# A state-space layer and a mixture of experts on one core: x1 on VectorE in the step of its output, experts chosen a step sooner

## The reference, cut to what matters

```python
z = irfft(rfft(x') * rfft(K)) + x' * D        # x' = layernorm(x); K is built from the S4D parameters
out = layernorm(x' + z) * ln_w + ln_b
x1 = x + layernorm(out)
zn = layernorm(layernorm(x1)) * ln_g + ln_b   # then the FFN
w = top-2 of softmax(zn @ rW + rb), over 8 experts
mixed = sum_e w_e * (gelu(zn @ W1_e + b1_e) @ W2_e + b2_e)
result = x1 + layernorm(layernorm(x1) + mixed)
```

## Time and profile before

| | |
|---|---|
| median of 3 runs | 642.32 us (641.46 to 644.99) |
| the profiled execution | 644.5 us, its span 642.9 us |
| granted TensorE clock, mean | 0.878 of full speed |
| busy in the span | PE 75%, VectorE 76%, ScalarE 51%, GpSimd 41% |

### The profile page before, as it was taken

How to read it: one execution, slowest core, us unless ns; L and a number is a source line. 1 busy time by engine, 2 the same in 40 slices (tenths; PEclk the granted TensorE clock), 3 DMA queues, 4 the chain that set the end, 5 groups by cost and what they waited for, 6 DMA issues and landing times. The chain is left out here.

```text
span 642.9 us, 12334 instructions
## 1 busy us (share of the span) xinstructions
PE 484.8 (75%) x2809; PEld 418.0 (65%) x2810; DVE 488.9 (76%) x1426; ACT 329.3 (51%) x646; POOL 262.4 (41%) x205
## 2 busy tenths in 40 slices
PE   0479899848997773600189999999999999992970
PEld 0239888736876663600078888888888889892760
DVE  7997959889988977884057778777777787770796
ACT  6974721353455366620055555555555555545485
POOL 0001586545776665788503223322332323233420
PEclk9998999968987985555579999999999999995995
DMA  6106500100110657642432222222222222215963
GB/s 198 66 0 262 197 1 0 66 1 9 59 68 33 229 197 216 227 139 74 153 118 68 81 66 82 66 82 66 82 67 80 66 82 72 75 49 212 346 229 145
DMA packets 36826, 69.55 MB, mean 108 GB/s; under 512 B 7520, under 2 KB 23648, under 8 KB 36160
## 3 DMA queue, kind: packets, MB, share of 16 engines
q1 hardware_dynamic: 30320, 51.48, 24.3%
q0 software_dynamic: 6480, 17.77, 7.7%
HBM read 42.02 MB, written 27.21 MB: 108 GB/s over the span
## 5 line engine op out<-in xcount | busy, mean ns | idle before, releaser
L1165 POOL DMA_INDIRECT y_rows<-y_sb,dst x71 | 76.6, 1079 | 192.7 <-DVE y_sb L1056 149.9
L1340 PE MATMUL psum<-ws,z_hl 128*128 x426 | 119.8, 417 | 0.8 <-DVE z_hl L1033 0.8
L1359 PE MATMUL psum<-ws,h_hl 128*128 x852 | 116.0, 286 | 0.1
L1359 PEld LDWEIGHTS psum<-ws,h_hl 128*128 128x128 f32 x852 | 103.6, 189 | 0.3 <-issue 0.3
L1147 POOL DMA_INDIRECT z_rows<-zn,pos x64 | 76.9, 1201 | 30.6 <-issue 17.7
L1340 PEld LDWEIGHTS psum<-ws,z_hl 128*128 128x128 f32 x426 | 76.7, 192 | 16.0 <-issue 1.5
L591 ACT CAST h_hl<-psum 128x512 fp32r<-128x512 f32 x71 | 41.7, 587 | 75.8 <-PE psum L1349 75.8
L1041 DVE TENSOR_TENSOR hb<-psum,b1r 128x512 f32<-128x512 f32 x71 | 49.1, 691 | 37.5 <-issue 34.0
L583 ACT ACTIVATE z_f<-psum,gb 128x128 f32<-128x128 f32 x142 | 57.0, 452 | 32.8 <-PE psum L1327 31.1
L1232 PE MATMUL psum<-pm,ft 128*128 128x256 f32 x256 | 65.7, 418 | 0.4 <-DVE tmp L836 0.4
L1327 PE MATMUL psum<-ident,z_in 128*128 128x128 f32 x142 | 28.6, 284 | 43.9 <-DMA z_in<-z_rows 42.0
(11 more groups left out here) (200 smaller groups left out, 874.7 us busy)
## 6 DMA issues: line engine op xcount, KB each, us to landing
z_in<-z_rows SPq DMA_DIRECT2D x71, 129.0 KB, 2.1
w_raw<-in_dram SPq DMA_DIRECT2D x16, 512.0 KB, 4.9
ya<-y_rows SPq DMA_DIRECT2D x16, 512.0 KB, 6.1
xs<-in_dram SPq DMA_DIRECT2D x8, 512.0 KB, 5.4
x_dram<-xs SPq DMA_DIRECT2D x8, 512.0 KB
x1m<-x_dram SPq DMA_DIRECT2D x2, 2048.0 KB, 8.4
out_dram<-acc SPq DMA_DIRECT2D x8, 512.0 KB, 2.6
b1r<-in_dram SPq DMA_DIRECT2D x8, 256.0 KB
```

The lines of the kernel that those rows point to most:

```text
L1165: pool.indirect_dma_start(y_rows, bass.IndirectOffsetOnAxis(ap=dst[q][:, 0:1], axis=0), y_sb[q][:, :], None).then_inc(sem(f"y_out{q}"), 16)
L1340: last = TE.matmul(ps_h[q], z_hl[q][:, a, k], w_at(e1, c, k * F, F), start=n == 0, stop=n == 5)
L1359: last = TE.matmul(ps_y[q], h_hl[q][:, a, k], w_at(e2, c, 1024 + k * H, H), start=n == 0, stop=n == 11)
```

## The change

- **x1** is made on VectorE in the step of its output: four `scalar_tensor_tensor` of 256 columns compute o*rs + x and at once sum their result into `st` (`accum_out`). The additive term (mean of o times rs) isn't applied there; it is kept in `xb` and added in the mixing stage by one more small operation per row. `dl` on ScalarE and the addition on GpSimd (L1139) go.
- **Statistics** of o and x1: the sums come with the operation that writes them (the addition of ln_b becomes four such operations too); the squares about the mean are summed by ScalarE (`ACT.Square` with `accum_out`, four per tensor). The eight bn_stats and eight bn_aggr per row for these two go. Those of r stay.
- **Routing a step sooner**: zn is written in the step of x1, tail is n-2. `choose` stands at the end of a step, `place` and the ranks in the next one, behind the statistics of r; in step 8 both follow for row 6 at once, and row 7 is chosen in step 9. rb and the regions' starts are added by two small TensorE matmuls; `lgs`, `posf`, `posr` go, and the copy of `tok` moves to ScalarE.
- **GpSimd**: the second half of `combine` moves to the start of the next step, the first waits for o; five scatters stand before it, three behind.
- **Weights**: the casts and subtractions move (the tables below); GpSimd makes none. A Gelu on one element is put before the tile loop on ScalarE.
- **SP**: the wait for the last scatters moves behind the pads.

```diff
@@ SP @@
             behind = [sp.value_load(padi[0:1, e:e + 1], min_val=0, max_val=ROWS - P) for e in range(E)]
-            for i in (2, 3):
-                sp.wait_ge(sem(f"scattered{i}"), 128)
             for e in range(E):
                 sp.dma_start(z_rows[bass.ds(behind[e], P), :], zpad[:, :]).then_inc(sem("pads"), 16)
...
             sp.wait_ge(sem("pads"), 16 * E)
+            for i in (2, 3):
+                sp.wait_ge(sem(f"scattered{i}"), 128)
             load_z(0, 0)
@@ ScalarE: renormalise, step @@
-                sigma(mid, 3)
-                act.wait_ge(sem("st_x1"), mid.b + 1)
+                act.wait_ge(sem("x1_mean"), row.b + 1)
+                for k in range(4):
+                    last = nc.scalar.activation(dump[:, k], xs[row.b][:, k], ACT.Square, bias=mv1[:, row.b, k, 0:1],
+                                                accum_out=mv1[:, row.b, k, 1:2])
+                last.then_inc(sem("var3"), 1)
+                sigma(row, 3)
+                act.wait_ge(sem("st_x1"), row.b + 1)
...
-                if n == B:
-                    renormalise(mid)
+                for e in HIGH.get(n, ()):
+                    split_high(e)
                 if cur.live:
-
+                    act.wait_ge(sem("o_mean"), cur.b + 1)
+                    for k in range(4):
+                        last = nc.scalar.activation(dump[:, k], o[:, k], ACT.Square, bias=mv[1][:, k, 0:1],
+                                                    accum_out=mv[1][:, k, 1:2])
+                    last.then_inc(sem("var1"), 1)
                     sigma(cur, 1)
-                    act.wait_ge(sem("st_o"), cur.b + 1)
-                    if not cur.first():
-                        act.wait_ge(sem("x1_ready"), cur.b)
-                    for k in range(4):
-                        last = nc.scalar.activation(dl[:, k], o[:, k], ACT.Identity, bias=rs[:, 1, 4 + k:5 + k],
-                                                    scale=rs[:, 1, k:k + 1])
-                    last.then_inc(sem("dl_ready"), 1)
...
-                if mid.live and n != B:
-                    renormalise(mid)
-                for e in HIGH.get(n, ()):
-                    split_high(e)
+                if cur.live:
+                    renormalise(cur)
@@ VectorE: step @@
+                if last_tail.live and n != B + 1:
+                    place(last_tail)
...
                 if n == B:
-                    mid_now()
+                    choose(tail)
...
-                    do(V.tensor_tensor(o[:, :, :], o[:, :, :], lwb[:, 1].unsqueeze(1).to_broadcast([P, 4, H]), ALU.add))
-                    stats(lambda k: o[:, k], 1)
+                    for k in range(4):
+                        last = V.scalar_tensor_tensor(o[:, k], o[:, k], 1.0, lwb[:, 1], ALU.mult, ALU.add,
+                                                      accum_out=st[:, 1, 0, k:k + 1])
+                    last.then_inc(sem("o_ready"), 1)
+                    dve.wait_ge(sem("o_ready"), cur.b + 1)
+                    V.tensor_scalar(mv[1][:, :, 0], st[:, 1, 0, 0:4], -1.0 / H, None, ALU.mult).then_inc(sem("o_mean"), 1)
                 if nxt.live:
                     mult(nxt, 1)
+                if n == B:
+                    place(tail)
                 if cur.live:
                     do(inverse(cur, 1))
...
+                    for k in range(4):
+                        last = V.scalar_tensor_tensor(xs[cur.b][:, k], o[:, k], rs[:, 1, k:k + 1], xs[cur.b][:, k], ALU.mult,
+                                                      ALU.add, accum_out=st[:, 3, 0, k:k + 1])
+                    last.then_inc(sem("x1_ready"), 1)
...
+                if tail.live and n != B:
+                    choose(tail)
+                if cur.live:
+                    do(inverse(cur, 3))
+                    V.tensor_tensor(rs[:, 3, 4:8], mv1[:, cur.b, :, 0], rs[:, 3, 0:4], ALU.mult).then_inc(sem("st_x1"), 1)
@@ VectorE: scale, in the mixing stage @@
-                       ALU.mult).then_inc(sem("m_rs"), 1)
+                       ALU.mult).then_inc(sem("m_sh"), 1)
+                dve.wait_ge(sem("m_sh"), b + 1)
+                gate(dve)
+                V.tensor_tensor(rm[:, par, 2, :], rm[:, par, 2, :], xb[:, bass.ds(back(b), 1)].rearrange("p a k -> p (a k)"),
+                                ALU.add).then_inc(sem("m_rs"), 1)
@@ GpSimd: step @@
+                if cur.live and cur.b:
+                    if cur.b > 1:
+                        pool.wait_ge(sem("st_x1"), cur.b - 1)
+                    combine(cur, 1)
+                if last_tail.live and n != B + 1:
+                    scatter(last_tail, 0, 5)
                 if nxt.live:
+                    if nxt.b > 1:
+                        pool.wait_ge(sem("o_ready"), nxt.b - 1)
                     combine(nxt, 0)
-                    combine(nxt, 1)
+                    if nxt.b == 0:
+                        combine(nxt, 1)
+                if last_tail.live and n != B + 1:
+                    scatter(last_tail, 5, 8)
+                if n == B:
+                    scatter(tail, 0, 8)
...
-                if cur.live:
-                    pool.wait_ge(sem("dl_ready"), cur.b + 1)
-                    G.tensor_tensor(xs[cur.b][:, :, :], xs[cur.b][:, :, :], dl[:, :, :], ALU.add).then_inc(sem("x1_ready"), 1)
@@ the tables @@
-HIGH = {3: (0,), 4: (1,), 5: (2,), 6: (3,), 7: (4,), 9: (5,), 10: (6,)}
-LOW = {9: (0,), 10: (1,), B + LAG: (4, 5, 6, 7)}
-LOW_POOL = {B + LAG: (2, 3)}
+HIGH = {0: (0, 1), 1: (2,), 4: (3,), 7: (4,), 8: (5, 6)}
+LOW = {1: (0, 1), 2: (2,), 8: (3,), 9: (4, 5, 6), B + LAG: (7,)}
```

More of the change, by code:

```diff
@@ L872, in place @@
                 for c in range(2):
[L873 removed]
+                    last = V.tensor_tensor(prod[:, c], oh[:, c], route(row.b)[1][:, 64:96].rearrange("p (t e) -> p t e", t=4),
+                                           ALU.mult)
                 do(last)
[L875 removed]
                 if not row.first(2):
                     dve.wait_ge(sem(f"scattered{row.par}"), 64 * min(row.b - row.par, 6))
[L878 removed]
@@ L879, in place @@
                 V.tensor_copy(zn[buf(row.b)][:, :, H + 1], mif[:, 1])
-                V.tensor_copy(pos[row.par][:, :, :], posr[:, :, :]).then_inc(sem("pos_ready"), 1)
+                with nc.allow_low_precision(reason="one term of each sum is not zero, and it is a whole number"):
+                    V.tensor_reduce(pos[row.par][:, :, :], prod[:, :, :, :], AX.X, ALU.add).then_inc(sem("pos_ready"), 1)
             def step(n):
-                nxt, cur, mid, tail = (Row(n, k) for k in (1, -1, -2, -LAG))
@@ L884, in mid_statistics @@
-                def mid_statistics():
-                    for k in range(4):
-                        last = V.bn_aggr(mv1[:, mid.b, k, :], st[:, 3, k, :])
-                    last.then_inc(sem("var3"), 1)
-                def mid_scales():
-                    if not mid.first():
-                        dve.wait_ge(sem("zn_ready"), mid.b)
-                    do(inverse(mid, 3))
-                    V.scalar_tensor_tensor(rs[:, 3, 4:8], mv1[:, mid.b, :, 0], -1.0, rs[:, 3, 0:4], ALU.mult,
-                                           ALU.mult).then_inc(sem("st_x1"), 1)
@@ L1277, in step @@
             def step(n):
-                nxt, cur, tail = Row(n, 1), Row(n, 0), Row(n, -LAG)
+                nxt, cur, tail, last_tail = (Row(n, k) for k in (1, 0, -2, -LAG))
+                if last_tail.live:
+                    pe.wait_ge(sem("mask_ready"), last_tail.b + 1)
+                    rank = route(last_tail.b)[1][:, 64:96]
+                    m = mask[:, :, :].rearrange("p t e -> p (t e)")
+                    TE.matmul(rank.rearrange("p (t e) -> p t e", t=4), ident[:, :],
+                              iota8[:, 1].unsqueeze(1).to_broadcast([P, 4, E]), start=True, stop=False)
+                    TE.matmul(rank, upper[:, 0, :], m, start=False, stop=False)
+                    for q in range(1, 4):
+                        TE.matmul(rank[:, q * E:4 * E], upper[:, 1, :], m[:, 0:(4 - q) * E], start=False, stop=False)
+                    if not last_tail.first():
+                        pe.wait_ge(sem("carry_ready"), last_tail.b)
+                    TE.matmul(rank.rearrange("p (t e) -> p t e", t=4), upper[:, 1, :],
+                              carry_b[:, :].unsqueeze(1).to_broadcast([P, 4, E]), start=False,
+                              stop=True).then_inc(sem("rank_mm"), 1)
                 if nxt.live and nxt.b:
                     fwd(nxt, 0)
-                if tail.live and tail.b < B - 1:
+                    fwd(nxt, 1)
+                if tail.live:
                     turn(tail)
-                if nxt.live and nxt.b:
-                    fwd(nxt, 1)
                 if cur.live:
```

118 lines of the change are left out of this document (36 added, 82 removed).

## The result

The changed kernel took **621.8 us** (median of 4 runs, 619.89 to 623.85), the kernel before beside it 643.65 us: a ratio of 0.966, 95% interval 0.961 to 0.971. In a second set of runs it was 624.5 us (620.39 to 627.15) at a ratio of 0.972 (0.965 to 0.978). The profiled execution, to which the sum of the prediction was made, took 619.89 us; forecast 620.2. For the median the forecast was 618, 3.8 us under what was measured. The profiled execution was the fastest of its four; the one traced in the second set was the slowest of its four, 627.15 us. The terms are less even than their sum.

What follows compares the result with a forecast made beforehand. VectorE was taken to set the late steps, GpSimd's scatters the chain behind them. Gains of 7.1, 11.2 and 8.0 less 2.0 gave 24.3 us: 644.5 to 620.2 profiled, 618 us median, range 604 to 634.

Steps and rivals of the forecast that it cites:

- Term 1: Pipeline steps: VectorE loses work, late steps fall from 22.24 to 20.0 us, so step 8 starts 7.1 us sooner.
- Term 2: Step 8 to the last scatter: 62.4 us become 51.2, a gain of 11.2 us.
- Term 3: SP's queue, last scatter to first tile: pads written during row 7's scatters, 12.8 us become 4.8, gain 8.0.
- Term 4: Mixing stage: one more small operation and wait per row, 2.0 us lost in all, bounds 1.3 and 10.
- two-step loop: Late steps: mask, TensorE, copy of s, then squares of x1 make two steps 38.6 us; restart up to 2.8.
- Half rate: Rival: VectorE's accumulating operations each cost 0.28 us more, +16 us in all, 634 us; chance 0.12.
- More is won: Rival: clock stays up, sums' read-out is free, steps of 18.4 to 19.0 us, 608 us in all; chance 0.12.
- The port: Rival: GpSimd's combine blocks VectorE's two-SBUF-input operations for x1 and o, 5.0 us a step, 653 us; chance 0.04.

Runs made afterwards that it cites:

- three edits: Changed kernel with x1 squared ahead of the copy of s, step 8's output ahead of row 6's choice, and scatters split four and four: 610.1 us, ratio 0.948.

## Why the prediction was right, point by point

The sum, 24.3 us, met the 24.6 between the two profiled executions because errors cancelled, which is luck. Term 1 gave 2.5 us more than forecast, term 2 0.6 more, term 3 0.1 less, and term 4 cost 2.6 more. The second trace of the same kernel is only 17.4 us under the kernel before: there term 1 gives 4.5 and term 3 6.8. The mechanisms of terms 1 and 3 are shown by runs. In term 2 one step of the reasoning fell, and term 4 was sized too small.

- **Term 1.** Late steps: forecast 20.0, the mean of steps 3 to 6 is 20.08 (20.7 in the second trace). The two-step loop is there, at 18.5 and 21.3 to 22.0, with a restart of 1.7 to 2.6 us. The run with the squares first shows that its cause is the one named: ScalarE's queue. Three errors lie below the sum. In two short steps the product L916 takes 1.75 us beside GpSimd, which I had counted at nothing. The idle times before the roots, where TensorE isn't late, are 0.35 and 0.7 for 0.7 and 1.3. And steps 1, 2 and 7 took 57.8 us together, where I had walked 59.9. Together with 0.8 us ahead of the first step, step 8 came 9.6 us sooner and not 7.1. The second trace, with 2.8 us more ahead of the first step and a lower clock (0.90), has 4.5: this term varies most.
- **Term 2.** 50.6 us; forecast 51.2. The scatter is held for 2.2 us as forecast (3.42 to 1.22), but the step that charged it to the path failed: two runs without it began to load z, counted from row 7's first scatter, 0.2 to 0.6 us sooner at most. The Trainium skill, "SBUF — State Buffer", section "Who interferes with whom", infers that a tensor_tensor leaves descriptor generation alone. The rows say otherwise, 3.42 us beside it and 1.22 without; for the time its nought was nearer, but because the landing behind the scatters comes at nearly the same time either way, not because the scatter was left alone.
- **Term 3.** 12.8 to 4.9 us; forecast 4.8. With the wait put back it was 12.05.
- **Term 4** was mis-sized. 8 x 0.25 was charged; the addition cost 3.6 to 4.2 us, within the stated bounds of 1.3 and 10. The link from one small operation to the next, which depends on it, is 0.45 us from start to start, not 0.16 and 0.1, and some rows lose more where VectorE's large addition then starts late (0.51 us at 592.85).
- **Half rate** is refuted by the rows of the long step shown first: 0.35 and 0.41 us per 256 columns, where it asked for over 0.6. The halved throughput that the Trainium skill states, "Vector Engine (DVE) Microarchitecture Reference", section "Points that are easy to get wrong", was not seen in these float32 operations.
- **More is won** had its condition half met: the clock rose from 0.87 to 0.94, but the steps stayed uneven. With three edits the kernel came to 610 us.
- **The port** had right what happens and what it costs VectorE in a step, 4.9 us for 5.0. The traces show only that VectorE's operations on two SBUF inputs stand still until GpSimd's tensor_tensor are over. Over seven steps 23.5 us were lost, not 35, since a wait of 4 us went with it in every other step. What stands against it is what the prediction named, the two waits; the loss showed with both taken away, and not with the wait for o alone. I had expected less than 3 us of that run, because GpSimd's order seemed to keep the collisions away by itself. A small part of it was in the changed kernel all along, at the place that the prediction named: the five scatters push the combination beside L916 in two short steps, 1.6 us each.

## To carry to other kernels

Where work with two SBUF inputs is moved onto VectorE while GpSimd runs tensor_tensor, waits that look useless on GpSimd can hold the whole gain, 23 us here: price the change with and without them, step by step. Where the steps of a loop are long and short in turn, look for a piece in an engine's queue that waits for TensorE ahead of one that doesn't. And count a new link in a chain of small dependent operations by the distance of two starts in the trace, not by the operation's own duration.

## What was not expected of the hardware

- A 256-column accumulation on VectorE that meets two back-to-back tensor_tensors of GpSimd waits for both: 3.26 us, where each of GpSimd's takes 1.27.
- Reading out an accumulator costs 0.08 us on VectorE, beside the next operation. On ScalarE it is 0.19 us, also beside it: four squares with their sums take 2.07 us (193.01 to 195.08), as four plain activations do (2.08).
- A held scatter may be issued 2.2 us later and the data behind it still be readable at nearly the same time (15.8 and 16.0 us after the first scatter). The profile puts the wait ahead of the load down to a scatter's landing in both (4.9 and 5.1 us); what makes that landing as late without the hold was not settled.
